# Layer norm's mean on VectorE instead of GpSimd, and the weight casts issued after the transposed reads

## What is computed

```python
xn = _layernorm(x)                       # (x - mean) / sqrt(var + eps), over the features
s  = attn(xn, qw, kw, vw, ow)            # rope, 16 heads of 64, causal softmax, output projection
gate_logits = xn @ Wg.T                  # 8 experts
vals, sel = top_k(gate_logits, 2); w = softmax(vals)
y = einsum('td,eod->teo', xn, We) + be   # We: 8 x 1024 x 1024 float32
g = silu(sum_k w_k * y[sel_k])
x = x + s * g
```

## Time and profile before

| | before |
|---|---|
| runs | 3209.33, 3214.8, 3343.53 us |
| median | 3214.8 us |
| profiled execution: its own time | 3209.84 us |
| its span, slowest core (core 1) | 3208.3 us |
| spans of all cores | 3186.7 to 3208.3 us |
| busy on core 1: PE, DVE, ACT, POOL | 2151.5, 1035.7, 939.9, 557.5 us |
| mean granted TensorE clock | 0.875 of full speed on core 1 |

### The profile page before, as it was taken

The page is one execution under the profiler, slowest core; times in us unless marked ns, Lnnn a source line. Parts: engine busy times, 40 slices in busy tenths (PEclk is TensorE's granted clock), DMA queues, the critical chain, the costliest instruction groups (busy, mean ns, idle before and its releaser), DMA issues.

```text
span 3208.3 us, 29319 instructions; the slowest of 8 cores (3186.7 to 3208.3 us)
## 1 busy us (share of the span) xinstructions
PE 2151.5 (67%) x9720; PEld 797.4 (25%) x9720; DVE 1035.7 (32%) x1368; ACT 939.9 (29%) x1245; POOL 557.5 (17%) x639
## 2 busy tenths in 40 slices
PE   0000038888839978995995997276778825777787
PEld 0000033333314433442442443021212111111212
DVE  2530035666634432441441443032221112221212
ACT  3430002222210010002002001246567704557575
POOL 1210005888730000000000000022111102111110
PEclk9999999999969988997997998577888865788888
DMA  4259922223365315707335631620201061220100
GB/s 122 92 100 112 139 46 66 99 100 103 109 114 90 53 38 95 104 1 131 53 53 91 93 53 43 169 66 1 66 1 53 1 151 35 66 59 7 53 1 27
DMA packets 418114, 229.07 MB, mean 71 GB/s; under 512 B 376480, under 2 KB 376480, under 8 KB 417456
## 3 DMA queue, kind: packets, MB, share of 16 engines
q1 hardware_dynamic: 403184, 159.54, 24.8%
q0 software_dynamic: 14784, 67.66, 9.4%
HBM read 92.67 MB, written 75.76 MB: 52 GB/s over the span
## 4 chain that ended last, share of the span: by engine, by line
PE 43%; DVE 11%; ACT 10%; DMA 9%; SPq 9%; issue 8%; POOL 5%; another core or an unknown queue 4%; POOLq 0%; DVEq 0%; ACTq 0%
PE PA L632 14%; PE PB L632 14%; SPq L238 8%; ACT AR L816 8%; PE PV L735 5%; POOL AR L827 4%; PE PA L861 4%; DMA AR<-c_sin 3%; DMA AR<-x_c 3%; PE PA L806 2%; PE PB L806 2%; DVE AR L528 2%; DVE AR L534 2%; DVE AR L526 2%
## 5 line engine op out<-in xcount | busy, mean ns | idle before, releaser
L632 PE MATMUL PA<-AR 128*128 128x512 f16 x2048 | 470.6, 383 | 34.0 <-DMA AR<-we 34.0
L632 PE MATMUL PB<-AR 128*128 128x512 f16 x2048 | 462.9, 379 | 0.0
L735 PE MATMUL PV<-AR 128*128 128x512 f16 (+6 forms) x1280 | 416.9, 416 | 66.3 <-POOL AR L827 66.1
L816 ACT ACTIVATE AR<-PA 128x1024 f16<-128x1024 f32 x320 | 303.5, 948 | 250.5 <-PE PA L806 248.4
L806 PE MATMUL PA<-AR 64*128 64x512 f16 x640 | 149.0, 456 | 295.2 <-ACT AR L816 142.3
L642 DVE SCALAR_TENSOR_TENSOR AR<-PA,wm,AR 128x512 f32<-128x512 f32 x256 | 192.2, 751 | 435.3 <-PE PA L632 222.9
L827 POOL TENSOR_TENSOR AR<-AR,tri 128x256 f16<-128x256 f16 x256 | 170.7, 667 | 818.1 <-ACT AR L816 794.2
L816 ACT ACTIVATE AR<-PB 128x1024 f16<-128x1024 f32 (+1 forms) x320 | 276.9, 865 | 90.1 <-PE PB L806 89.8
L381 PE MATMUL PC<-wgT,AR 128*128 128x8 f16 x768 | 25.5, 166 | 369.7 <-DMA AR<-xn_sp 369.7
L642 DVE SCALAR_TENSOR_TENSOR AR<-PB,wm,AR 128x512 f32<-128x512 f32 x256 | 192.2, 751 | 249.3 <-PE PB L632 233.0
L632 PEld LDWEIGHTS PA<-AR 128*128 128x128 f16 x2048 | 202.2, 99 | 282.2 <-issue 45.9
(11 more groups left out here) (95 smaller groups left out, 1837.9 us busy)
## 6 DMA issues: line engine op xcount, KB each, us to landing
we<-we POOLq DMA_DIRECT2D x8, 2048.0 KB, 91.9
out_c<-AR SPq DMA_DIRECT2D x8, 2048.0 KB, 9.2
v_sp<-AR POOLq DMA_DIRECT2D x32, 264.0 KB, 3.2
AR<-v_sp POOLq DMA_DIRECT2D x2, 4224.0 KB, 25.2
AR<-x_c POOLq DMA_DIRECT2D x32, 256.0 KB, 3.0
xn_sp<-AR SPq DMA_DIRECT2D x32, 256.0 KB, 2.5
AR<-c_cos SPq DMA_DIRECT2D x32, 256.0 KB, 2.8
AR<-c_sin SPq DMA_DIRECT2D x32, 256.0 KB, 3.1
```

The costliest lines, as they stand in the source:

```text
L632: sl=slots[ib], half=half: e.matmul(PG[:, 512 * ib:512 * ib + 512], lhs, sl[:, c * D + half * 512: c * D + (half + 1) * 512], start=(c == ...
L735: nkc=nkc, p2=p2, mw=mw: e.matmul(PV2[0:mw, 512 * p2 + w0:512 * p2 + 512], v_sb[:, kc * VF + h * VW:kc * VF + h * VW + mw], expb3[sbk][:, ...
L816: W("scalar", lambda e, PS=PS, sbk=sbk, ev=ev: e.activation(ev(expb3[sbk]), ev(PS), AF.Exp, scale=1.0 / 32.0), waits=[("eT", C["eT"]), ("e ...
```

## The change

Two edits. The two 128x1 operations that make the mean and its negative move from POOL to DVE, with their semaphore, so that POOL's list in the layer norm holds the loads of x alone, and ACT waits on DVE for `mneg`. And the nine DMAs of the weight casts and the bias move behind the transposing reads in program order; the first of them waits, on POOL, until all eight reads have landed.

```diff
-            W("gpsimd", lambda e, q=q: e.tensor_scalar(
+            W("vector", lambda e, q=q: e.tensor_scalar(
                 m16[q][:, :], m32[q][:, :], 1.0 / D, None, op0=ALU.mult),
-              waits=[("eV", C["eV"]), ("eP", C["eP"])], inc="eP")
-            W("gpsimd", lambda e, q=q: e.tensor_scalar(
+              waits=[("eV", C["eV"])], inc="eV")
+            W("vector", lambda e, q=q: e.tensor_scalar(
                 mneg[q][:, :], m16[q][:, :], -1.0, None, op0=ALU.mult),
-              waits=[("eP", C["eP"])], inc="eP")
-            tok[("mnegd", q)] = C["eP"]
+              waits=[("eV", C["eV"])], inc="eV")
+            tok[("mnegd", q)] = C["eV"]
...
-              waits=[("eP", tok[("mnegd", q)]),
+              waits=[("eV", tok[("mnegd", q)]),
                      ("eV", tok.get(("xc16", q), 0))], inc="eA")
...
-        for ei in range(NE):
-            dma("gpsimd", we16[ei, :, :], we_h[ei, :, :], "swe")
-        dma("gpsimd", be16s[0:8, :], be_h[:, :], "sbe")
-
...
         xnT_rd = C["sxnT"]
+
+        dma("gpsimd", we16[0, :, :], we_h[0, :, :], "swe",
+            waits=[("sxnT", xnT_rd)])
+        for ei in range(1, NE):
+            dma("gpsimd", we16[ei, :, :], we_h[ei, :, :], "swe")
+        dma("gpsimd", be16s[0:8, :], be_h[:, :], "sbe")
```

## The result

The changed kernel takes 3108.7 us (median) against 3204 to 3215 us for the kernel before: a ratio of 0.9686 with a 95% interval of 0.9674 to 0.9699, 3.1% faster. The profiled execution took 3108.71 us, its span is 3107.2 us, so 101.1 us less than in the profile before. The forecast was 3079 us with 3055 to 3112 as its range. The measured median of 3108.7 lies just inside these limits, but as a ratio to the median that the forecast named (0.9686 x 3214.8 = 3113.9 us) it lies just outside: 101 us came of the 131 forecast, so nearly a quarter of the gain is missing.

What follows compares the result with a forecast made beforehand. Bound by two DMA stretches end to end with nothing beside them, after a layer norm slowed by waiting loads. 44 us from the layer norm's turns plus 87 from the casts, 130.9 off 3209.84, gave 3079 us, range 3055 to 3112.

Steps and rivals of the forecast that it cites:

- The layer norm: Layer norm loop: loads no longer wait for sums, a turn falls from 5.60 to 4.08 us, 44 us gained.
- The start: Layer norm's beginning: does not move, as DVE waits for ACT's gate weights up to the sum at 50.70 us.
- The reads stay as long: Transposing reads after the layer norm: start at 178 us, still take 46.7 us, end at 224.7.
- The casts stay as long: Weight casts behind the reads: issued at 225 us, still take 159.8 us, end at 384.8.
- Under them lie the gating and the projection of tile 0: During the casts: gating and tile 0's projection run alongside; the casts' part of the gain is 87 us.
- nothing changes behind the second rope: After tile 1's rope starts at 388.2 us: all as before, so its 130.9 us gain reaches the end.
- The tables of tile 1 wait for the casts' end: Tile 1's cosine and sine tables: land 3.4 us after the casts end, at 388.2 us.
- The gating is undisturbed by the casts: Gating beside the casts: starts at 224.7 us, first rope follows 88.3 us later, at 313, as before.
- nothing is hidden under the casts: Rival on gating and tile 0: a transfer sticks, projection begins only at 385 us, total 3104 us; chance 0.05.
- The clock: Rival in the experts' stage: granted clock falls from 0.91 to attention's 0.77, total 3248 us; chance 0.02.
- the quick passage: Rival beside the casts: small transfers pass within a few turns, tile 1 finishes under them, total 3066 us; chance 0.06.
- 38 us a store: Stores beside the casts: 128 rows of 2 KB take 38 us, one row a turn, 4.8 us a turn.

Runs made afterwards that it cites:

- e3: Changed kernel with GpSimd marking the first barrier by a 128x1 memset, not a drain: 0.9626 of the kernel before, 0.9615 when run again.
- after_again: The changed kernel unaltered, run once more on the same chip as the repeat of e3: 0.9689 of the kernel before.
- e10: Against e3, cosine and sine tables issued one tile ahead, before the store of q: 0.9403 of the kernel before, 2999.8 to 3004.4 us.
- e5: Against e3, every cast's rows walked with a stride, so each descriptor holds one row (2 KB written): 0.9643 of the kernel before, about 3095 us.
- e4: Against the changed kernel, four of eight casts stay before the first barrier, four move behind it with the bias, drain kept: 3085.5 us in one run.

## Why the prediction was right and wrong

- **The layer norm:** right in mechanism and size. 4.10 us a turn against 4.08. The start was taken as fixed and is not: POOL now issues four loads of x at once at 1.6 us (2.33 us in one row, where the kernel before issues one), SP's loads of the weights take longer beside them, the gate weights' load is issued at 19.8 and not at 16.7 us, and everything behind it is 2.3 us later. These are 2.3 of the 4 us by which the reads start late, at 182.0 and not at 178.
- **The reads stay as long:** right, 182.0 to 230.4 = 48.4 us against 46.7.
- **The casts stay as long:** right. Issued at 231, the bias landed at 387.1; 384.8 was forecast.
- **"Under them lie the gating and the projection of tile 0":** this step failed. The gating does lie there, the projection does not, because the barrier between them has a drain of GpSimd, and the casts were GpSimd's. The step named GpSimd's queue for the stores of k and v and passed over the one instruction in it that stands directly behind the casts. Its price: from the bias' landing to the second rope it took 416.8 - 387.1 = 29.7 us where 3.4 was forecast, 26.3 us of the 28.6 by which the second rope is late. e3 took the drain away and had the second rope at 386.4, within 2 us of the forecast's 388.2. Even so, its ratio of 0.9615 to 0.9626 is 3086 to 3090 us on the forecast's scale and not 3079: that nothing changes behind the second rope held for the changed kernel (102.3 us earlier there, 101.1 at the end), but not for e3 (25 us earlier than after_again at the second rope and 18 at the end), and why is open.
- **The tables of tile 1 wait for the casts' end:** right, but behind the drain it never came to bear; e3 shows it (35.4 us), and e10, where the tables do not wait, has the second rope right behind the first.
- **The gating is undisturbed by the casts:** wrong, and without effect on the changed kernel. It ended 98.6 us after its start and not 74 us; of that, 28.8 us are five gaps of TensorE between blocks of 128 to 180 matmuls, in which it waits for nothing that the profile shows:

```profile
230.66 5.41 PE L383 MATMUL PC<-wgT,AR 128*128 128x8 f16 x180 [181.32 <-DMA AR<-xn_sp]
240.87 3.63 PE L383 MATMUL PC<-wgT,AR 128*128 128x8 f16 x128 [4.80 <-issue]
250.63 3.63 PE L383 MATMUL PC<-wgT,AR 128*128 128x8 f16 x128 [6.13 <-issue]
```

  In the kernel before the same 768 matmuls take 26.4 us without a gap. The instruction queue moves one transfer of some 16 KB in each of the five gaps, at 238.5, 248.0, 257.5, 267.0 and 276.5 us to within half a microsecond, and TensorE goes on 2 to 3 us behind each. In the kernel before, six such transfers lie in the 26.4 us, one every 4.5 us, and no gap. So instructions that are fetched late beside the casts fit well; as no run took the fetches away, this is argued and not shown. Smaller pieces of cast left the gaps nearly as they were (one of 0.7 us and four of 5.0 to 5.9 in e5), so the piece's size is not what sets them.
- **The rivals:** "nothing is hidden under the casts", 3104 us, is what happened in time (projection from 389 us, 385 in the rival), though it was given 0.05 and put down to a transfer that sticks. The clock stayed: 0.91 and 0.77 in the last two stages, as before.
- **The rule of the Trainium skill** (page "DMA: Bandwidth & Descriptors", section "Queues, rings and completion order") is that an engine drains a whole packet of some 9 to 17 descriptors at a turn. The 38.7 us of the store of q in e4, which landed with 16 us of casts still to come, and the tables' 34 to 35 us in e3 and 55 to 56 us in e4, all at the casts' end, speak against the quick passage that the prediction read out of it, and for the 38 us a store that it took from the row.

The sign and the chances for it stand; the size missed by nearly a quarter because one row of the kernel before, the drain's 158 us, was left out of account. The range went 8 us beyond the rival's 3104 us, and the measured ratio lies 2 us beyond that.

## What to carry to other kernels

Before work is moved beside a long transfer, list every instruction behind the transfer on the queue that issues it, drains and barriers first: here a drain on GpSimd waited for GpSimd's own DMAs and passed the wait on to all engines, and it had shown as a 158 us row already where it cost nothing. If transfers are to run across a barrier that only orders engine work, GpSimd should raise its mark by an operation in its order and not by a drain; the readers of the transfers must then wait on the transfers' own semaphores, as the experts' stage does here. And what repeats in each turn is worth more than what happens once: issuing the tables one tile ahead, against a wait of 4 us in each of 32 turns, brought about three times what taking the drain away did (68 us against some 20).

## What the runs showed of the hardware

- GpSimd's drain lasts until its DMAs have landed: 78.0 us with four casts under way, 154.4 us with eight, and in the kernel before and the changed one it ends 1.7 us behind the last landing; a memset at the same place passes at once.
- GpSimd's issue of a DMA can stand: with 1024 rows a cast, seven went out in 7.5 us, the next one 135 us later; eight with two of them in the large pieces went out in 7.4 us.
- Beside casts that fill the DMA engines, a 256 KB transfer of 2 KB rows takes 33 to 42 us with the large pieces, and 55 to 56 where it stands behind another in its queue (e4); with 2 KB pieces a store landed in 11.4 us and the tables queued behind it in 15.6 and 20.2, against 2 to 4 us alone.
- TensorE's stream had gaps of mostly 5 to 6 us every 128 matmuls while casts ran, with large and with small pieces, and in the changed kernel each gap held one transfer of the instruction queue.
